# Householder tridiagonalisation: another order for the steps of the last four 128-column blocks

## The chip, the core and the metric

One NeuronCore of a Trainium2 chip runs the whole program; the other cores are idle. The metric is the device time of one execution in microseconds (us). TensorE (PE) multiplies, VectorE (DVE), ScalarE (ACT) and GpSimd (POOL) work elementwise; engines synchronise by semaphores, and each engine takes its own instructions in the order in which they are written.

## The reference

Four graph layers run one after another over `x` (8 x 1024 x 128), each behind a layer norm and relu. The third needs all eigenvectors of a 1024 x 1024 normalised Laplacian:

```
deg = jnp.sum(A, axis=0) + jnp.sum(A, axis=1) - jnp.diagonal(A)
d_inv_sqrt = jnp.where(deg > 0, jax.lax.rsqrt(deg), 0.0)
L = jnp.diag(deg) - A
L_norm = d_inv_sqrt[:, None] * L * d_inv_sqrt[None, :]
_, U = jnp.linalg.eigh(L_norm)
agg = jnp.einsum('mn,bnd->bmd', U.T, features)
h = jax.nn.relu(agg @ W1 + b1)
out = h @ W2 + b2
return jnp.einsum('nm,bmd->bnd', U, out)
```

The other layers are a graph convolution with batch norms, and two attention layers. `eigh` is done in the kernel: reduction to a tridiagonal matrix, eigenvalues by multisection, eigenvectors of the tridiagonal matrix, back transformation.

## The kernel before, in words

The change lies in `tridiagonalise` alone. It removes one column per step with a Householder reflection, 1023 columns, one after another. The matrix `A` stays in SBUF, 128 rows per partition group. Columns go in eight blocks of 128 (`b` = 0 to 7); `T = NT - b` is the number of 128-row tiles that are still active, so T is 8 in the first block and 4, 3, 2, 1 in the last four. A block has four panels of 32 columns (`s` = 0 to 31, `NB_P`); within a panel the matrix itself is not touched, and corrections from the panel's earlier reflections are added instead. At a panel's end TensorE turns the stored vectors and a rank-64 product updates the matrix (L325 to L333, L511 to L518).

Each step is a chain through four engines, held together by semaphores that count steps. In the order of the chain, for the four last blocks:

- `X` (L487) is the new column, and it starts a step. L490 writes the previous step's vector `w`.
- The norm: L430 sums the squares of X per partition into `part`; TensorE sums over partitions with a matrix of ones into `sigma` (in `ring[1]`); ScalarE takes the root, `mu` (L364).
- Scalars (DVE): `rt` = 1/mu, `fl`, `S2` (L449), `pair` (L454), `inv` (L459), `s4` (L468).
- Between them stand the corrections for s > 0: TensorE reads one row of the stored vectors (`rows`) and multiplies X with them (`coefs`); DVE forms `prodb`, `rowsum`, `BnS`, `prodc`, `corr`. Their sizes grow with s.
- The product: TensorE multiplies the matrix with X, `y` (L289, `product(t)` for each tile t), DVE turns it with `tr` (L437) and adds `corr`, which is `t1`, called `tm` (L473).
- Kappa: L476 multiplies `tm`, the scale `s4` and `gx` and sums along the row into `kp`; TensorE sums over the partitions (`kappa`, and `c_sum` once more).
- The end: DVE forms `qa`, `z` (L481), `q` (L483), and with kappa the next X (L487). POOL forms fB, nB and Bc, and ScalarE `sM` and `vm` beside it.

A helper `four` issues each small matmul for four groups of 32 output columns. In the profile each of these counts twice, so one group is x8. The matmuls on `ident16` (L314) write to a bank that nobody reads; there are 8 of them in a step with T = 6 and 10 with T of 5 or less. They stand in TensorE's order between the product and kappa.

```
early = 0 if T < 4 else 1
...
for _ in range(8 if T == 6 else 10):
    nc.tensor.matmul(ring[3][:, 0:P], S["ident16"][:, :], S["ident16"][:, :], start=True, stop=True)
```

Of the kernel before, what the change touches and what calls it, by code (L numbers as in the profile page):

```python
# [11 lines left out]
P = 128  # L12
# [156 lines left out]
XC = N + 5 * NB_P + 1  # L169


def tridiagonalise(nc, S):
# [3 lines left out]
    with ExitStack() as ctx:  # L176
# [11 lines left out]
        eS = sb("eS", [P, NB_P]); tauS = sb("tauS", [P, NB_P]); dS = sb("dS", [P, NB_P]); dq = sb("dq", [P, NB_P]); DS = sb("DS", [P, N])  # L188
# [26 lines left out]
        last_body = len(bodies) - 1  # L215

# [18 lines left out]
        def _(pool):  # L235
# [9 lines left out]
            for k, (b, it0, cnt, s0, s1) in enumerate(bodies):  # L245
                T = NT - b
                with pool.Fori(0, cnt) as it:
                    pool.wait_ge(window_ready, it + (panels_before[k] + 1))
                    for s in range(s0, s1):
# [5 lines left out]
                        pool.wait_ge(Bn_ready, r + 1)  # L255
                        nc.gpsimd.tensor_scalar(fB[:, b:NT], col, fl[:, s:s + 1], None, ALU.mult).then_inc(pool_step, 1)  # L256
                        pool.wait_ge(pool_step, 3 * r + 1)
                        nc.gpsimd.tensor_tensor(nB[:, b:NT], fB[:, b:NT], col, ALU.subtract).then_inc(pool_step, 1)
                        pool.wait_ge(pool_step, 3 * r + 2)
                        nc.gpsimd.tensor_tensor(Bc[:, b:NT], nB[:, b:NT], half_M[:, s, 0:T], ALU.mult).then_inc(pool_step, 1)  # L260
# [5 lines left out]
        def _(pe):  # L266
# [9 lines left out]
            for k, (b, it0, cnt, s0, s1) in enumerate(bodies):  # L276
                T = NT - b
                with pe.Fori(0, cnt) as it:
# [3 lines left out]
                    for s in range(s0, s1):  # L282
# [14 lines left out]
                        early = 0 if T < 4 else 1  # L297
                        for t in range(early):
                            product(t)
# [9 lines left out]
                        for t in range(early, T):  # L309
                            product(t)  # L310
                        if T <= 6:

                            for _ in range(8 if T == 6 else 10):
                                nc.tensor.matmul(ring[3][:, 0:P], S["ident16"][:, :], S["ident16"][:, :], start=True, stop=True)  # L314
                        pe.wait_ge(kappa_part, r + 1)
                        four(kappa(s), half[:, 0:32], kp[:, :]).then_inc(kappa_ready, 1)
                        four(c_sum, half[:, 0:32], kp[:, :], stop=False)
# [28 lines left out]
        def _(act):  # L346
            act.wait_ge(low_ready, 7)
            for k, (b, it0, cnt, s0, s1) in enumerate(bodies):
                T = NT - b
                with act.Fori(0, cnt) as it:  # L350
# [10 lines left out]
                    for s in range(s0, s1):  # L361
# [3 lines left out]
                        act.wait_ge(s4_ready, r + 1)  # L365
                        nc.scalar.activation(sM[:, b:NT], half_M[:, s, 0:T], ACT.Copy, scale=s4[:, s:s + 1]).then_inc(sM_ready, 1)  # L366
# [18 lines left out]
        def _(dve):  # L385
# [14 lines left out]
            for k, (b, it0, cnt, s0, s1) in enumerate(bodies):  # L400
                T = NT - b
                act_t = slice(b, NT)
                with dve.Fori(0, cnt) as it:
# [1573 lines left out]
```

## Time and profile before

| | us |
|---|---|
| Median of 3 runs | 9805.91 (9801.75 to 9810.02) |
| The profiled execution | 9792.26 |
| Its span | 9790.5 |
| Mean granted TensorE clock, whole span | 0.746 of 2.4 GHz |
| DVE busy | 7098.8 (73%) |
| PE busy, modelled | 5600.1 (57%) |

The tridiagonalisation takes the span from about 908 to 6007 us; the last four blocks begin at 3863.1 us. In the rows, the first number of a timeline row is its start in us from the start of the span, and the second its duration; L numbers are lines of the kernel. PE rows are matmuls, PEld their weight loads.

### The profile page before, as it was taken

The numbers are of one execution on the slowest core, as the hardware profiler recorded it, in microseconds if no ns is written. First come the engines' busy times: TensorE is split into PE (matmuls) and PEld (weight loads), VectorE is DVE, ScalarE is ACT, GpSimd is POOL, SyncE is SP. The second block draws the span as 40 slices with busy tenths as digits, with TensorE's granted clock in tenths as the row PEclk, the third lists the DMA queues.
The fourth block names the chain that finished last, engine by engine and source line by source line (L and its number), as shares of the span: only waits on it lengthen the run. The fifth ranks groups of instructions, "written<-read, shape, count | busy, mean of one in ns | idle before, by whom it ended". The sixth has DMA issues, their size and how long they took to land. (4 is left out here: it accounts for less than half of the span.)

```text
span 9790.5 us, 326141 instructions
## 1 busy us (share of the span) xinstructions
PE 5600.1 (57%) x136408; PEld 3949.5 (40%) x136408; DVE 7098.8 (73%) x33446; ACT 1776.4 (18%) x4691; POOL 1185.3 (12%) x5177
## 2 busy tenths in 40 slices
PE   5675888777878777778777764121111110047866
PEld 2354555555566666566656653010000000033355
DVE  3555666767777777777777778989898989954154
ACT  1432111111111111111111111121111110011055
POOL 0000111111222222222222221000000000000000
PEclk8898999999999999786655555555555555579988
DMA  1000000000000000000000000000000000000000
GB/s 35 1 0 18 4 4 4 4 4 4 4 4 4 4 4 4 4 4 4 4 4 4 3 3 2 0 0 0 0 0 0 0 0 0 0 0 1 17 0 17
DMA packets 24594, 41.92 MB, mean 4 GB/s; under 512 B 2464, under 2 KB 20128, under 8 KB 23200
## 3 DMA queue, kind: packets, MB, share of 16 engines
q8 instruction: 1074, 17.60, 0.8%
q1 hardware_dynamic: 23200, 21.70, 0.7%
q14 instruction: 320, 2.62, 0.1%
HBM read 17.50 MB, written 4.19 MB: 2 GB/s over the span
## 5 line engine op out<-in xcount | busy, mean ns | idle before, releaser
L289 PE MATMUL tri_y<-L 128*32 128x256 f32 (+7 forms) x36792 | 1941.3, 343 | 18.7 <-issue 17.7
L289 PEld LDWEIGHTS tri_y<-L 128*32 128x32 f32 x36792 | 1187.9, 122 | 241.9 <-issue 66.3
L1342 PE MATMUL ev_agree<-ev_prod,ev_fold 128*128 128x448 bf16 x520 | 241.3, 567 | 1683.5 <-DVE ev_prod L1465 1666.9
L1342 PEld LDWEIGHTS ev_agree<-ev_prod,ev_fold 128*128 128x128 bf16 x520 | 34.8, 111 | 1887.8 <-DVE ev_prod L1465 1867.4
L314 PE MATMUL tri_ring<-ident 128*128 128x128 bf16 x7414 | 750.3, 268 | 2.1 <-issue 1.9
L1458 DVE SCALAR_TENSOR_TENSOR ev_seq<-ev_seq,ev_ne2G,ev_u 128x112 f32<-128x112 f32 x2048 | 686.1, 335 | 73.3
L1454 DVE SCALAR_TENSOR_TENSOR ev_u<-ev_x,ev_dG,ev_seq 128x112 f32<-128x112 f32 x2048 | 683.9, 334 | 64.0
L272 PE MATMUL tri_k<-tri_kp,tri_half 128*32 128x1 f32 x8176 | 264.8, 189 | 759.7 <-DVE tri_x L476 755.8
L364 ACT ACTIVATE tri_mu<-tri_ring,tri_tiny 128x1 f32<-128x1 f32 x1022 | 267.4, 262 | 2172.6 <-PE tri_ring L272 2172.6
L314 PEld LDWEIGHTS tri_ring<-ident 128*128 128x128 bf16 x7414 | 582.1, 121 | 171.0 <-issue 155.6
L366 ACT ACTIVATE tri_sM<-tri_half_M,tri_s 128x8 f32<-128x8 f32 (+7 forms) x1022 | 304.2, 298 | 1823.4 <-DVE tri_s L468 1823.4
L272 PE MATMUL tri_ring<-L 128*32 128x32 f32 (+25 forms) x35704 | 597.8, 206 | 0.0
L272 PEld LDWEIGHTS tri_k<-tri_kp,tri_half 128*32 128x32 f32 x8176 | 177.6, 120 | 1040.4 <-DVE tri_x L476 1038.8
L256 POOL TENSOR_SCALAR tri_fB<-tri_BnS,tri_fl 128x8 f32<-128x8 f32 (+7 forms) x991 | 303.1, 306 | 2262.2 <-DVE tri_BnS L462 2262.2
L1323 ACT ACTIVATE ev_sgn<-ev_seq 128x1008 bf16<-128x1008 f32 x256 | 267.0, 1043 | 1703.0 <-DVE ev_dummy L1472 1703.0
L440 DVE RECIPROCAL tri_rt<-tri_mu 128x1 f32<-128x1 f32 x1022 | 167.2, 164 | 544.5 <-ACT tri_mu L364 544.5
L437 DVE STREAM_TRANSPOSE tri_tr<-tri_y 128x256 f32<-128x256 f32 (+7 forms) x1022 | 333.7, 326 | 300.6 <-PE tri_y L289 298.2
L272 PEld LDWEIGHTS tri_ring<-L 128*32 128x32 f32 x35704 | 514.4, 118 | 0.2
L272 PE MATMUL tri_p<-L,tri_Hw 128*32 128x2 f32 x8176 | 265.6, 189 | 329.5 <-DVE L L487 188.2
L254 POOL TENSOR_TENSOR tri_xm<-L,tri_Mw 128x8 f32<-128x8 f32 (+7 forms) x1022 | 214.2, 210 | 1404.3 <-DVE L L487 1072.0
L272 PEld LDWEIGHTS tri_p<-L,tri_Hw 128*32 128x32 f32 x8176 | 177.5, 119 | 440.1 <-DVE L L487 278.9
L487 DVE SCALAR_TENSOR_TENSOR L<-tri_vm,tri_k,tri_q 128x8 f32<-128x8 f32 (+7 forms) x1022 | 235.7, 231 | 160.4 <-PE tri_k L272 68.2
(615 smaller groups left out, 12957.9 us busy)
## 6 DMA issues: line engine op xcount, KB each, us to landing
adj<-in_adj_dram SPq DMA_DIRECT2D x12, 1024.0 KB, 8.1
x<-in_x_dram SPq DMA_DIRECT2D x8, 512.0 KB, 7.2
out_dram<-x SPq DMA_DIRECT2D x8, 512.0 KB, 6.6
gcn_w<-in_L_gnn_W_dram SPq DMA_DIRECT2D x2, 128.0 KB, 2.1
spec_w<-in_L_gnn_W_dram SPq DMA_DIRECT2D x2, 64.0 KB, 1.9
dot_wt<-in_L_gnn_W_dram SPq DMA_DIRECT2D x1, 64.0 KB, 1.8
dot_rows<-in_L_gnn_b_lin_dram SPq DMA_DIRECT2D x1, 64.0 KB, 2.7
dot_rows<-in_L_gnn_b_dram SPq DMA_DIRECT2D x1, 64.0 KB, 3.7
```

Of the source, the lines that this page charges most:

```text
L256: nc.gpsimd.tensor_scalar(fB[:, b:NT], col, fl[:, s:s + 1], None, ALU.mult).then_inc(pool_step, 1)
L272: last = nc.tensor.matmul(out[32 * g:32 * g + 32, :], lhsT, rhs, start=start, stop=stop)
L289: last = nc.tensor.matmul(y[32 * g:32 * g + 32, 0:T * 32], A[:, b + t, XC:XC + 1].broadcast_to([P, 32]), cols, start=(t == 0), stop=(t == ...
L314: nc.tensor.matmul(ring[3][:, 0:P], S["ident16"][:, :], S["ident16"][:, :], start=True, stop=True)
L364: nc.scalar.activation(mu[:, :], sigma, ACT.Sqrt, bias=tiny[:, :]).then_inc(root_ready, 1)
L366: nc.scalar.activation(sM[:, b:NT], half_M[:, s, 0:T], ACT.Copy, scale=s4[:, s:s + 1]).then_inc(sM_ready, 1)
L437: return mark(V_.transpose(tr[:, 0:T * 32], y[:, 0:T * 32]))
L487: V_.scalar_tensor_tensor(out=X, in0=vm[:, act_t], scalar=kappa(s), in1=q[:, act_t], op0=ALU.mult, op1=ALU.subtract).then_inc(x_ready, 1)
L1323: nc.scalar.activation(sgn[:, y % 2, :, :], seq[:, y % 2, 1:GRP + 2, :], ACT.Sign).then_inc(sgn_done, 1)
L1342: last = nc.tensor.matmul(agree, fold16[:, :], prod[:, z, h * (GRP // 2):(h + 1) * (GRP // 2), :].rearrange("p s w -> p (s w)"), start=Fal ...
L1454: ku[c] = mark(V.scalar_tensor_tensor(out=u[:, h], in0=xw[:, h], scalar=dG[:, i:i + 1], in1=seq[:, z, s + 1, h], op0=ALU.subtract, op1=ALU ...
L1458: ins = V.scalar_tensor_tensor(out=seq[:, z, s + 2, h], in0=seq[:, z, s, h], scalar=ne2G[:, i:i + 1], in1=u[:, h], op0=ALU.mult, op1=ALU.add)
```

## The change

It touches steps with T of 4 or less (`few(T)`), 511 steps of 1023; code for larger T is as before. In these steps:

- Kappa is no longer summed along the row on DVE. TensorE multiplies `gx` with `tm` for each tile and accumulates, T groups in place of one, and the sum lacks the factor s4/2. That factor is in `vmc` (ACT, from `vm`), used in X, and at a panel's end in `kS`. `c_sum` is T groups of `gx` with `zh` (ACT: tm scaled by s4/2) and the one group with `z`.
- `sigma` is summed a second time, into `sigma_v` in kappa's bank, for DVE. `fl` and a new `sgn2` = sigma_v * sg read it, and stand ahead of `rt`. `aa` = mu * sg + pivot is new, `pair` = rt * sgn2 + aa, and `S2` is gone.
- The norm of the next step stands right behind X, ahead of `w`.
- The turn `tr` stands ahead of `gx` and `s4`. `s4` is two values wide.
- POOL forms `Cf` and `BnS`, DVE `fB`; q is made as (z - column) * half_M in two instructions behind z. `sM`, `nB`, `Bc` and `qa` are gone.
- On TensorE the first tile of the product stands ahead of rows and coefs, behind sigma and sigma_v; for T of 1 and 2 the whole product does. The `ident16` matmuls are 8, 10, 12, 12 for T = 4, 3, 2, 1.

The diff, cut to its core:

```
+FILL = {6: 8, 5: 10, 4: 8, 3: 10, 2: 12, 1: 12}
...
+        sigma_v = kbank[:, NB_P:NB_P + 1]
+        few = lambda T: T <= 4
...
@@ gpsimd
+                        if few(T):
+                            pool.wait_ge(fl_ready, r + 1)
+                            nc.gpsimd.tensor_scalar(Cf[:, b:NT], Cw[:, b:NT, s], fl[:, s:s + 1], None, ALU.mult).then_inc(Cf_ready, 1)
+                            if s:
+                                pool.wait_ge(sum_ready, r + 1 if s0 else r)
+                                nc.gpsimd.tensor_tensor(col, Cw[:, b:NT, s], rowsum[:, b:NT], ALU.add).then_inc(Bn_ready, 1)
...
@@ tensor
+                        first = T if T <= 2 else 1
+                        if not few(T):
+                            for t in range(first):
+                                product(t)
                         pe.wait_ge(norm_part, r + 1)
                         four(sigma, ones[:, 0:32], part[:, :]).then_inc(norm_ready, 1)
+                        if few(T):
+                            four(sigma_v, ones[:, 0:32], part[:, :]).then_inc(norm_again, 1)
+                            for t in range(first):
+                                product(t)
...
+                        if few(T):
+                            pe.wait_ge(gx_ready, r + 1)
+                            pe.wait_ge(t_ready, r + 1)
...
+                            for t in range(T):
+                                last = four(kappa(s), gx[:, b + t:b + t + 1].broadcast_to([P, 32]), tm[:, t0 + t:t0 + t + 1], start=(t == 0), stop=(t == T - 1))
+                            last.then_inc(kappa_ready, 1)
+                            pe.wait_ge(zh_ready, r + 1)
+                            for t in range(T):
+                                four(c_sum, gx[:, b + t:b + t + 1].broadcast_to([P, 32]), zh[:, b + t:b + t + 1], start=(t == 0), stop=False)
...
@@ scalar
+                        if few(T):
+                            act.wait_ge(s4_ready, r + 1)
+                            act.wait_ge(vm_ready, r + 1)
+                            nc.scalar.activation(vmc[:, b:NT], vm[:, b:NT], ACT.Copy, scale=s4[:, s, 1:2]).then_inc(vmc_ready, 1)
...
+                            act.wait_ge(t_ready, r + 1)
+                            nc.scalar.activation(zh[:, b:NT], tm, ACT.Copy, scale=s4[:, s, 1:2]).then_inc(zh_ready, 1)
```

DVE's side is shown by the order of its instructions. First the scalars of a step with T = 1, from `sg` on; before:

```order
L433 TENSOR_SCALAR tri_sg<-tri_p 128x1
L440 RECIPROCAL tri_rt<-tri_mu 128x1
L441 TENSOR_SCALAR tri_fl<-tri_p,tri_ring 128x1
L445 TENSOR_TENSOR tri_prodb<-L,tri_r 128x4
L449 SCALAR_TENSOR_TENSOR tri_S<-tri_rt,tri_ring,tri_mu 128x1
L452 TENSOR_REDUCE tri_rowsum<-tri_prodb 128x1
L454 SCALAR_TENSOR_TENSOR tri_pair<-tri_S,tri_sg,tri_p 128x2
L457 TENSOR_TENSOR tri_prodc<-L,tri_ring 128x4
L459 RECIPROCAL tri_inv<-tri_pair 128x2
```

The same place on DVE after the change (L493 is `rt`, tri_sgn is sgn2):

```order
L487 TENSOR_SCALAR tri_sg<-tri_p 128x1
L489 TENSOR_SCALAR tri_fl<-tri_p,tri_k 128x1
L491 TENSOR_SCALAR tri_sgn<-tri_k,tri_sg 128x1
L493 RECIPROCAL tri_rt<-tri_mu 128x1
L494 SCALAR_TENSOR_TENSOR tri_aa<-tri_mu,tri_sg,tri_p 128x2
L497 TENSOR_TENSOR tri_prodb<-L,tri_r 128x6
L499 SCALAR_TENSOR_TENSOR tri_pair<-tri_rt,tri_sgn,tri_aa 128x2
L502 TENSOR_TENSOR tri_prodc<-L,tri_ring 128x6
L504 TENSOR_REDUCE tri_rowsum<-tri_prodb 128x1
L506 RECIPROCAL tri_inv<-tri_pair 128x2
```

`fl` moved ahead of `rt`, and rowsum behind prodc. Then the end of a step with T = 1 on DVE, from corr to X; before (tri_x, tri_kp is the kappa sum along the row):

```order
L464 TENSOR_REDUCE tri_corr<-tri_prodc 128x1
L468 TENSOR_SCALAR tri_s<-tri_inv,tri_fl 128x1
L469 SCALAR_TENSOR_TENSOR tri_gx<-L,tri_inv,tri_Hw 128x1
L437 STREAM_TRANSPOSE tri_tr<-tri_y 128x32
L473 TENSOR_TENSOR tri_t<-tri_tr,tri_corr 128x1
L476 SCALAR_TENSOR_TENSOR tri_x,tri_kp<-tri_t,tri_s,tri_gx 128x1
L479 TENSOR_TENSOR tri_qa<-tri_t,tri_sM 128x1
L481 SCALAR_TENSOR_TENSOR tri_zS<-tri_t,tri_s,tri_fB 128x1
L483 TENSOR_TENSOR tri_q<-tri_qa,tri_Bc 128x1
L487 SCALAR_TENSOR_TENSOR L<-tri_vm,tri_k,tri_q 128x1
```

The same place on DVE after the change, from corr over X to w (L470 is the norm, L548 is w):

```order
L509 TENSOR_REDUCE tri_corr<-tri_prodc 128x1
L511 STREAM_TRANSPOSE tri_tr<-tri_y 128x32
L517 SCALAR_TENSOR_TENSOR tri_gx<-L,tri_inv,tri_Hw 128x1
L519 SCALAR_TENSOR_TENSOR tri_s<-tri_one_half,tri_inv,tri_fl 128x2
L522 TENSOR_TENSOR tri_t<-tri_tr,tri_corr 128x1
L525 SCALAR_TENSOR_TENSOR tri_fB<-tri_rowsum,tri_fl,tri_Cf 128x1
L533 SCALAR_TENSOR_TENSOR tri_zS<-tri_t,tri_s,tri_fB 128x1
L537 TENSOR_TENSOR tri_q<-tri_zS,tri_BnS 128x1
L539 TENSOR_TENSOR tri_q<-tri_q,tri_half_M 128x1
L543 SCALAR_TENSOR_TENSOR L<-tri_vmc,tri_k,tri_q 128x1
L470 ISA tri_x,tri_part<-L 128x1
L548 SCALAR_TENSOR_TENSOR L<-L,tri_ring,tri_zS 128x2
```

The kappa sum and qa are gone, fB and one of the two q instructions are new, and the norm stands ahead of w. Last, TensorE between the norm and the next step with T = 3; before:

```order
L272 MATMUL tri_ring<-L 32x18 x12
L289 MATMUL tri_y<-L 32x96 x12
L314 MATMUL tri_ring<-ident 128x128 x10
L272 MATMUL tri_k<-tri_kp,tri_half 32x1
L272 MATMUL tri_k<-tri_kp,tri_half 32x1 x3
L272 MATMUL tri_ring<-tri_kp,tri_half 32x1 x4
```

The same stretch of TensorE after the change, from the second sum of the norm on:

```order
L289 MATMUL tri_k<-tri_part,ones 32x1 x4
L306 MATMUL tri_y<-L 32x96 x4
L289 MATMUL tri_r<-L,tri_Hw 32x18
L289 MATMUL tri_r<-L,tri_Hw 32x18 x3
L289 MATMUL tri_ring<-L 32x18 x12
L306 MATMUL tri_y<-L 32x96 x8
L335 MATMUL tri_ring<-ident 128x128 x10
L289 MATMUL tri_k<-tri_t,tri_gx 32x1
L289 MATMUL tri_k<-tri_t,tri_gx 32x1 x11
L289 MATMUL tri_ring<-tri_zh,tri_gx 32x1
L289 MATMUL tri_ring<-tri_zh,tri_gx 32x1 x11
```

A third of the product stands earlier; kappa is 12 matmuls for 4, and c_sum has 12 with zh for the 4 with kp.

## Rows read from the trace of the kernel before

**Rows 1.** The page: the span and the granted clock in 40 equal slices.

```profile
span 9790.5 us, 326141 instructions
PEclk8898999999999999786655555555555555579988
```

**Rows 2.** Busy time in the four last blocks, T = 4, 3, 2, 1.

```profile
core 0: us, PE busy (x) PEld busy (x) DVE busy (x) ACT busy (x) POOL busy (x), PEclk, DMA share, GB/s
3863.10:4438.30 575.20, 435.99 (x15520) 343.99 (x15520) 449.30 (x3092) 103.38 (x427) 140.98 (x640) 0.83 0.02 4
4438.30:4983.30 545.00, 429.65 (x13488) 343.36 (x13488) 425.51 (x3088) 102.48 (x426) 138.62 (x640) 0.67 0.02 4
4983.30:5509.70 526.40, 409.45 (x11456) 327.54 (x11456) 401.59 (x3084) 101.59 (x427) 136.24 (x640) 0.50 0.01 4
5509.70:6007.00 497.30, 348.00 (x9354) 281.94 (x9354) 380.02 (x3059) 99.49 (x417) 132.40 (x635) 0.50 0.01 3
```

**Rows 3.** Timeline of one step, T = 1: start us, duration us, engine, line.

```profile
5700.21 0.22 DVE L487 SCALAR_TENSOR_TENSOR L<-tri_vm,tri_k,tri_q 128x1 f32<-128x1 f32 x1 [0.17 <-PE tri_k L272]
5700.64 0.14 DVE L430 CUSTOM_DVE_ANT_0 tri_x<-L 128x1 f32<-128x1 f32 x1
5700.85 0.29 PE L272 MATMUL tri_ring<-tri_part,ones 128*32 128x1 f32 x8
5701.20 0.26 ACT L364 ACTIVATE tri_mu<-tri_ring,tri_tiny 128x1 f32<-128x1 f32 x1 [1.68 <-PE tri_ring L272]
5701.50 0.16 DVE L440 RECIPROCAL tri_rt<-tri_mu 128x1 f32<-128x1 f32 x1 [0.49 <-ACT tri_mu L364]
5701.58 0.27 DVE L441 TENSOR_SCALAR tri_fl<-tri_p,tri_ring 128x1 f32<-128x1 f32 x1
5701.77 0.18 DVE L445 TENSOR_TENSOR tri_prodb<-L,tri_r 128x34 f32<-128x34 f32 x1
5701.86 0.22 DVE L449 SCALAR_TENSOR_TENSOR tri_S<-tri_rt,tri_ring,tri_mu 128x1 f32<-128x1 f32 x1
5702.12 0.22 DVE L454 SCALAR_TENSOR_TENSOR tri_pair<-tri_S,tri_sg,tri_p 128x2 f32<-128x2 f32 x1
5702.37 0.17 DVE L459 RECIPROCAL tri_inv<-tri_pair 128x2 f32<-128x2 f32 x1
5702.51 0.18 DVE L464 TENSOR_REDUCE tri_corr<-tri_prodc 128x1 f32<-128x34 f32 x1
5702.60 0.20 DVE L468 TENSOR_SCALAR tri_s<-tri_inv,tri_fl 128x1 f32<-128x1 f32 x1
5702.72 0.23 DVE L469 SCALAR_TENSOR_TENSOR tri_gx<-L,tri_inv,tri_Hw 128x1 f32<-128x1 f32 x1
5702.88 0.20 DVE L437 STREAM_TRANSPOSE tri_tr<-tri_y 128x32 f32<-128x32 f32 x1
5703.11 0.16 DVE L473 TENSOR_TENSOR tri_t<-tri_tr,tri_corr 128x1 f32<-128x1 f32 x1
5703.31 0.22 DVE L476 SCALAR_TENSOR_TENSOR tri_x<-tri_t,tri_s,tri_gx 128x1 f32<-128x1 f32 x1
5703.59 0.29 PE L272 MATMUL tri_k<-tri_kp,tri_half 128*32 128x1 f32 x8 [0.89 <-DVE tri_x L476]
5704.00 0.22 DVE L487 SCALAR_TENSOR_TENSOR L<-tri_vm,tri_k,tri_q 128x1 f32<-128x1 f32 x1 [0.16 <-PE tri_k L272]
```

**Rows 4.** Timeline of TensorE, T = 3, a step at half clock.

```profile
4455.49 1.25 PE L314 MATMUL tri_ring<-ident 128*128 128x128 bf16 x10
4456.67 0.29 PE L272 MATMUL tri_k<-tri_kp,tri_half 128*32 128x1 f32 x8
4457.91 0.49 PE L272 MATMUL tri_ring<-L 128*32 128x10 f32 x24
```

**Rows 5.** Timeline of TensorE, T = 2.

```profile
5161.89 0.63 PE L289 MATMUL tri_y<-L 128*32 128x64 f32 x16
```

**Rows 6.** Timeline of TensorE, T = 4, a step at full clock.

```profile
4352.80 0.73 PE L314 MATMUL tri_ring<-ident 128*128 128x128 bf16 x10
```

More of the change, by code:

```diff
@@ L308, in _ @@
                             last.then_inc(coefs_ready, 1)
[L309 removed]
+                        for t in range(first, T):
                             product(t)
[L311 to L317, printed above, removed]
+                        for _ in range(idle(T)):
+                            nc.tensor.matmul(ring[3][:, 0:P], S["ident16"][:, :], S["ident16"][:, :], start=True, stop=True)
+                        if few(T):
+                            pe.wait_ge(gx_ready, r + 1)
+                            pe.wait_ge(t_ready, r + 1)
+                            tm = t1 if s else tr[:, 0:NT * 32].rearrange("p (t m) -> p t m", m=32)[:, :, 0]
+                            t0 = b if s else 0
+                            for t in range(T):
[4 more added lines that the diff above has]
+                                four(c_sum, gx[:, b + t:b + t + 1].broadcast_to([P, 32]), zh[:, b + t:b + t + 1], start=(t == 0), stop=False)
+                        else:
+                            pe.wait_ge(kappa_part, r + 1)
+                            four(kappa(s), half[:, 0:32], kp[:, :]).then_inc(kappa_ready, 1)
+                            four(c_sum, half[:, 0:32], kp[:, :], stop=False)
                         pe.wait_ge(z_ready, r + 1)
@@ L448, in _ @@
-                        after(kk)
-                        kk = mark(V_.scalar_tensor_tensor(out=S2[:, :], in0=rt[:, :], scalar=sigma, in1=mu[:, :], op0=ALU.mult, op1=ALU.add))
-                        if s:
-                            after(k_b)
-                            k_b = mark(V_.tensor_reduce(rowsum[:, act_t], c3(prodb), mybir.AxisListType.XY, ALU.add))
-                        after(kk)
-                        kk = mark(V_.scalar_tensor_tensor(out=pair[:, s, :], in0=S2[:, :].broadcast_to([P, 2]), scalar=sg[:, :], in1=pivot(s), op0=ALU.mult, op1=ALU.add))
@@ L455, in _ @@
-                        if s:
-                            dve.wait_ge(coefs_ready, r + 1 if s0 else r)
-                            k_c = mark(V_.tensor_tensor(c3(prodc), v_w(b)[:, :, :, 0:s], spread(coefs(s)), ALU.mult))
-                        after(kk)
-                        V_.reciprocal(inv[:, :], pair[:, s, :]).then_inc(inv_ready, 1)
-                        if s:
-                            after(k_b)
-                            V_.tensor_tensor(BnS[:, s, 0:T], Cw[:, act_t, s], rowsum[:, act_t], ALU.add).then_inc(Bn_ready, 1)
-                            after(k_c)
-                            k_c = mark(V_.tensor_reduce(corr[:, act_t], c3(prodc), mybir.AxisListType.XY, ALU.add))
```

220 lines of the change are left out of this document (159 added, 61 removed).

## The prediction

> **What bounds the kernel now.** I read the page first for the slices, then busy time block by block, then the timeline of single steps. The page gives a span of 9790.5 us, and a clock row that is near full until about the twentieth slice and at half from the twenty-fourth [rows 1]. The four last blocks, the only ones touched, take 575.2 + 545.0 + 526.4 + 497.3 = 2143.9 us, 22% of the span, and the mean granted clock in them is 0.83, 0.67, 0.50 and 0.50 [rows 2]. As the clock has two levels, 1.2 and 2.4 GHz, the share of time at the lower one is 2 x (1 - mean): 0.34, 0.66, 1 and 1. So there are four blocks under three regimes, and I make the sum for each.
>
> In the last block (T = 1) a step runs from X at 5700.21 to the next X at 5704.00, 3.79 us [rows 3]. The reader is to see a chain with hardly a hole. X to norm takes 0.43 (w stands between), norm to sigma 0.21, sigma to the root 0.35, root to rt 0.30. From rt at 1.29 to kappa's row sum at 3.10, DVE issues one small instruction after another. Then kappa's matmul comes 0.28 after the row sum, and X 0.41 after the matmul. TensorE waits 0.89 for that row sum, so it has room here. Two kinds of distance matter below: an instruction that needs the one before it starts its duration + 0.04 later (t 0.16, next at +0.20; S2 0.22, pair at +0.26), one that doesn't starts 0.08 to 0.19 later (rt to fl 0.08, fl to prodb 0.19, s4 to gx 0.12, gx to tr 0.16) [rows 3].
>
> At T = 3 and half clock it is another picture: the ten idle matmuls begin at 4455.49, take 1.25, and kappa's matmul starts at 4456.67, in their wake [rows 4]. There TensorE's own queue is the path, and whatever is put ahead of kappa on TensorE is paid.
>
> **The new step, T = 1**, in us after X, by distances of [rows 3]. The norm is now directly behind X: 0.22 + 0.04 = 0.26. Sigma 0.47; sigma_v one group later. A group's distance I take from [rows 4]: 24 matmuls last 0.49 and 8 last 0.29, so 0.10 for each further group; with a little for the first, 0.12: 0.59. fl reads sigma_v 0.41 after its matmul (as X does kappa): 1.00. The root, at 0.82 + 0.30 = 1.12, is no longer what is waited for; fl is. Then sgn2 1.19, rt 1.31, aa 1.39, prodb 1.52, pair 1.65 (aa + 0.26), prodc 1.78, rowsum 1.90, inv 2.02, corr 2.10, tr 2.19, gx 2.34, s4 2.49, t 2.61, fB 2.70. The tail is now four dependent instructions: z 0.26 after fB, 2.96; first q 3.22; second q 3.42; X 3.62 (0.20 each behind a 0.16 tensor_tensor). Kappa's matmul would be at 2.61 + 0.28 = 2.89 and allow X at 3.30; vmc (s4 + 0.26, then a ScalarE instruction of about 0.30) allows it near 3.1. So kappa, for which the change is made, stops being the last wait, and the q chain takes its place; from t to X it was 0.89 and will be 1.01. The gain is made ahead of t: 3.79 - 3.62 = 0.17 to 0.20, since the steps that I took at 0.15 (tr to gx, gx to s4) may be 0.12. I take 0.19: 127 x 0.19 = -24 us. Bounds: nothing, if w (below) delays fl by 0.2, and 0.30, if z, q1 and q overlap more than rows of dependent pairs say.
>
> **T = 2, half clock.** The same chain, but both product tiles are now ahead of rows. Their 16 matmuls last 0.63 [rows 5]: sigma_v 0.59, product from 0.71, rows from about 1.30, with DVE 0.41 later at 1.71, where prodb could start at 1.52. That eats 0.17 to 0.19 of the 0.19, and with large s, where rows and coefs take longer, a little more. I take -0.02: 128 x 0.02 = -3 us; bounds -0.15 and +0.10.
>
> **T = 3.** At full clock TensorE has room and DVE's chain holds: -0.18. At half clock, where the path is TensorE's queue [rows 4]: sigma starts 0.12 earlier, sigma_v costs 0.12, the product's place changes nothing, and kappa is three groups instead of one, +0.24. In all +0.24. For large s DVE's corrections take over again (they grow with s) and the step gains 0.10. Half and half: +0.07. Sum: 84 steps x 0.07 = +6, 44 x -0.18 = -8: -2 us.
>
> **T = 4.** Full clock, 84 steps x -0.18 = -15. Half clock, 44 steps: sigma_v +0.12, three more kappa groups +0.34, two idle matmuls fewer -0.25 (1.25 / 10 each, [rows 4]; at full clock 0.73 / 10, [rows 6]), waiting for the norm where a product tile stood before +0.09: +0.30, 44 x 0.30 = +13. Sum -2 us. The case of T = 4 is an estimate from the T = 3 rows.
>
> **What is priced at nothing.** c_sum is late now: it waits for zh, which ScalarE makes after t. At T = 1 zh starts near 2.9, c_sum's groups run from 3.2 to 3.4, and w follows at X + 0.2, behind the norm, which is issued anyway. At T = 4 three more groups put w at X + 0.4 to 0.5; behind w stand sg and fl, and fl waits for sigma_v till 1.00, so 0.5 is covered; without this cover each 0.1 costs 0.1 a step. Rows on TensorE waits for w too, but stands behind a product tile. POOL's Cf and BnS have over 0.7 before they are read. kS and one more link at a panel's end: 16 x 0.07 = +1 us.
>
> **Sum**: -24 - 3 - 2 - 2 + 1 = -30 us. Against the profiled execution, 9792.3 becomes 9762; the median of the runs is 9805.9, 13.6 higher, and becomes 9776.
>
> A rule that weighs the change otherwise: the Trainium skill, "VectorE: DVE Perf Modes", under "The DRAIN you can't avoid", says that the next operation doesn't start until the pipe is empty, that semaphores between operations are free, and that only the number of operations counts. The rows differ: fl starts 0.08 after an rt that lasts 0.16, and a dependent successor 0.20 after t [rows 3]. By the rule the q chain would cost no more than independent instructions, and one instruction fewer a step (the row sum's second half goes) would be worth about 0.08 x 511 = -41 us by itself.
>
> **Rivals.**
> *A, the clock rises.* A step has more matmuls (sigma_v, kappa, c_sum; two more idle ones at T of 1 and 2) in less time. If T = 4 and 3 stay at full clock, the 44 steps at T = 4 gain 0.48 (from +0.30 to -0.18) and the 0.4 that they are now longer than their full-clock neighbours (most of the 0.52 between 1.25 and 0.73 for the idle matmuls, [rows 4, 6]): -39. The 84 at T = 3 gain 0.25 to 0.3: -23. Together -30 - 62 = -92: 9714. For it: the clock already changes level inside these two blocks [rows 2]. Against: T = 3 has TensorE busy for 430 of 545 us at mean clock 0.67, and T = 2 for 409 of 526 at 0.50 [rows 2], so being busy doesn't raise it by itself, and small matmuls may count little. The Trainium skill, "TensorE: Matmul & The Clock Gate", under "The HAM clock gate", has the clock throttled by default and released by activity; by it A would be the expected outcome wherever TensorE's idle time shrinks.
>
> *B, slower: TensorE's queue at T = 4.* Two idle matmuls fewer may tip the block to half clock. Each step that changes from full to half costs 0.48 + 0.4 = 0.88. All 84: +74; the 44 of T = 3: +12; so +86 - 30 = +56: 9862. It decides against the change from 30 / 0.88 = 34 steps on, that is when the share at half clock at T = 4 goes from 0.34 to 0.61. For it: kappa already follows the idle matmuls without a gap [rows 4]. Against: the shorter full-clock step (4%) restores the density that they took away.
>
> *C, no gain.* Either w binds, since fl now stands behind it on DVE and comes ahead of rt, or the new waits cost what was saved. The 0.18 at full clock and at T = 1 shrink to 0 to 0.05: the sum is 0 to -8, or +19 where the half-clock costs (+6, +13) stay: 9798 to 9825, centre 9808. For it: the free time ahead of fl is an inference, as no row shows c_sum with several groups.
>
> **Chances.** Forecast 0.50, A 0.20, B 0.12, C 0.18. A measurement of this kernel can tell 0.2%, 20 us, from no change. Of the forecast's 0.50, whose own range is 9750 to 9795, about 0.07 lies within 20 us; of C 0.12 lies within it and 0.06 above. So faster 0.43 + 0.20 = 0.63, same 0.19, slower 0.18. The range goes from 9705 to 9825: it holds A down to its centre and C, and leaves out most of B.
>
> **What would show it.** In the profile after: norm about 0.26 after X; fl near 1.0 and ahead of rt, with DVE idle before fl (waiting for PE) instead of before rt (waiting for ACT); at T = 1 kappa's matmuls well before X, and DVE's wait on kappa ahead of X gone, the q chain in its place; a step at T = 1 of 3.60 to 3.62 and a last block of about 473 us; at T = 2 prodb waiting for rows, the block at about 524; clocks of 0.83 and 0.67 in the first two. I am wrong if the clock in any block moves by more than 0.05, if X still waits for kappa at T = 1, or if w delays fl.

## The result, and the profile after

The changed kernel takes 10035.51 us (median of 4 runs, 10021.51 to 10055.83), the kernel before 9803.83 beside it: ratio 1.0242, 95% interval 1.0218 to 1.0266. It is slower by 232 us. The forecast was 9776, its range 9705 to 9825.

The page after, to be held against [rows 1]: 240.0 us more span, 11% more instructions, and a clock that falls one slice earlier (the 16th).

```profile
span 10030.5 us, 360888 instructions
PE 5987.8 (60%) x153038; PEld 4340.2 (43%) x153038; DVE 7186.2 (72%) x32953; ACT 1928.3 (19%) x5202; POOL 1093.0 (11%) x4650
PEclk8898999999999997666655555555555555579978
```

Busy time of the four last blocks after, which answers to [rows 2]:

```profile
3855.30:4626.80 771.50, 621.17 (x22432) 507.70 (x22432) 484.60 (x2968) 141.52 (x554) 116.04 (x508) 0.64 0.02 4
4626.80:5254.50 627.70, 527.15 (x18608) 437.07 (x18608) 452.71 (x2964) 140.47 (x553) 115.45 (x508) 0.59 0.02 4
5254.50:5773.40 518.90, 467.52 (x14784) 412.10 (x14784) 419.42 (x2960) 139.58 (x555) 114.02 (x508) 0.50 0.02 4
5773.40:6253.00 479.60, 398.99 (x10636) 332.46 (x10636) 385.48 (x2938) 136.87 (x544) 109.89 (x504) 0.50 0.01 4
```

Measured from the start of one block to that of the next, T = 4 went from 575.1 to 771.5 (+196.4), T = 3 from 545.0 to 627.8 (+82.8), T = 2 from 526.4 to 518.8 (-7.6), T = 1 from 502.6 to 480.0 (-22.6). A block whose code is the same in two kernels varies between profiles: by 25 us at T = 5 (611.8 to 636.9), by under 8 us at T of 4 and below. So the two last blocks did what was forecast (-3, -24), and the loss is all in the first two (forecast -2 and -2). The DVE column grows little there; what grows is TensorE's count of instructions: (22432 + 22432) / 128 = 350 a step at T = 4, where [rows 2] give 243. The granted clock went from 0.83 to 0.64 at T = 4 and from 0.67 to 0.59 at T = 3.

TensorE's timeline after, T = 4, in the record that answers to [rows 6]:

```profile
4111.21 0.43 PE L289 MATMUL tri_k<-tri_t,tri_gx 128*32 128x1 f32 x32
4112.69 0.41 PE L306 MATMUL tri_y<-L 128*32 128x128 f32 x8
4114.08 0.62 PE L335 MATMUL tri_ring<-ident 128*128 128x128 bf16 x8
4115.06 0.23 PE L289 MATMUL tri_k<-tri_t,tri_gx 128*32 128x1 f32 x4 [0.36 <-DVE tri_t L522]
4115.91 0.39 PE L289 MATMUL tri_k<-tri_t,tri_gx 128*32 128x1 f32 x26 [0.62 <-issue]
4116.93 0.24 PE L289 MATMUL tri_ring<-tri_part,ones 128*32 128x1 f32 x8
4117.36 0.38 PE L289 MATMUL tri_ring<-L 128*32 128x24 f32 x20
4119.65 0.36 PE L289 MATMUL tri_ring<-L 128*32 128x24 f32 x10 [1.92 <-issue]
4119.89 1.47 PE L306 MATMUL tri_y<-L 128*32 128x128 f32 x22
```

The reader is to see the last but one row. Coefs is 32 matmuls in a row on one wait; after 20 of them TensorE does nothing for 1.92 us and then goes on with the same operation. No semaphore stands there, and the trace names no releaser ("issue"). The same happens inside kappa at 4115.91. I counted such stretches (over 0.3 us, within a TensorE operation or with no releaser) over a block's panels: 84 at T = 4, 111.8 us in all; 65 at T = 3, 67.6 us; none in either block before. I call them dry stretches. The other engines wait for them, as the waits of the T = 4 block show (engine, line, what it waited for, us in total, times, longest):

```profile
DVE tri_tr L511 <- PE tri_y L306: 88.2, 109, 2.6
PE tri_ring L289 <- issue: 47.6, 32, 1.9
DVE tri_prodc L502 <- PE tri_ring L289: 46.7, 41, 2.1
```

The first row isn't made of dry stretches alone: DVE's turn `tr` waits for the product in 109 steps, more than there are stretches. In the same block before it hardly waited:

```profile
DVE tri_tr L437 <- PE tri_y L289: 1.2, 7, 0.2
```

What runs dry can be read from the DMA view. The queue "q8 instruction" brings TensorE's instructions from memory: in e3_pad84 below, where nothing but TensorE instructions was added to the kernel before, the T = 1 block had 153 of its packets for 76. In the T = 4 block (the columns are packets, MB, share of 16 engines) it brought after, in 737 us:

```profile
q8 instruction: 176, 2.88, 1.6%
```

and before, in 575 us:

```profile
q8 instruction: 126, 2.06, 1.5%
```

A packet is 16.4 KB, and by 31040 matmuls and loads for 126 packets it holds some 250 of them. A step with 352 needs 1.4 packets. In the stretch of the timeline above they began at 4105.6, 4109.5, 4113.5, 4117.4, 4121.3, 4125.3 and 4128.6 and took about 1 us each: one every 3.4 to 4.0 us, where 84 instructions a us would need one every 3.0.

At T = 1 the new step is much as forecast; to be held against [rows 3]:

```profile
5951.34 0.22 DVE L543 SCALAR_TENSOR_TENSOR L<-tri_vmc,tri_k,tri_q 128x1 f32<-128x1 f32 x1
5951.60 0.16 DVE L470 CUSTOM_DVE_ANT_0 tri_x<-L 128x1 f32<-128x1 f32 x1
5952.28 0.28 DVE L489 TENSOR_SCALAR tri_fl<-tri_p,tri_k 128x1 f32<-128x1 f32 x1 [0.16 <-PE tri_k L289]
5952.61 0.15 DVE L493 RECIPROCAL tri_rt<-tri_mu 128x1 f32<-128x1 f32 x1
5953.76 0.15 DVE L522 TENSOR_TENSOR tri_t<-tri_tr,tri_corr 128x1 f32<-128x1 f32 x1
5954.05 0.29 PE L289 MATMUL tri_k<-tri_t,tri_gx 128*32 128x1 f32 x8
5954.10 0.22 DVE L533 SCALAR_TENSOR_TENSOR tri_zS<-tri_t,tri_s,tri_fB 128x1 f32<-128x1 f32 x1
5954.51 0.16 DVE L537 TENSOR_TENSOR tri_q<-tri_zS,tri_BnS 128x1 f32<-128x1 f32 x1 [0.19 <-DVE tri_zS L533]
5954.71 0.16 DVE L539 TENSOR_TENSOR tri_q<-tri_q,tri_half_M 128x1 f32<-128x1 f32 x1
5955.00 0.22 DVE L543 SCALAR_TENSOR_TENSOR L<-tri_vmc,tri_k,tri_q 128x1 f32<-128x1 f32 x1
```

The norm is 0.26 after X, fl 0.94 and ahead of rt and waiting for TensorE, kappa's matmul 0.95 before X, and the q chain is last (X shows no wait). The mean step at T = 1 inside the panels is 3.57 us (3.79 before; 3.62 forecast).

### The profile page after: what moved, and what is told of

Read it like the earlier page. It is cut to its first block and busy times, and to the rows that moved or that the text cites. A ratio compares the mean times of both kernels' runs of the same rounds, so it can differ in the third digit from the quotient of the medians.

```text
span 10030.5 us, 360888 instructions
## 1 busy us (share of the span) xinstructions
PE 5987.8 (60%) x153038; PEld 4340.2 (43%) x153038; DVE 7186.2 (72%) x32953; ACT 1928.3 (19%) x5202; POOL 1093.0 (11%) x4650
## 5 line engine op out<-in xcount | busy, mean ns | idle before, releaser
L306 PE MATMUL tri_y<-L 128*32 128x256 f32 (+7 forms) x36792 | 2053.5, 351 | 82.9 <-issue 82.0
L306 PEld LDWEIGHTS tri_y<-L 128*32 128x32 f32 x36792 | 1232.0, 125 | 315.0 <-issue 137.1
L335 PE MATMUL tri_ring<-ident 128*128 128x128 bf16 x7668 | 824.3, 280 | 20.4 <-issue 20.4
L335 PEld LDWEIGHTS tri_ring<-ident 128*128 128x128 bf16 x7668 | 645.8, 127 | 195.8 <-issue 175.6
L404 ACT ACTIVATE tri_vm<-tri_xm,tri_inv 128x8 f32<-128x8 f32 (+7 forms) x1022 | 296.4, 290 | 772.1 <-DVE tri_inv L506 772.1
L557 DVE STREAM_TRANSPOSE tri_tr<-tri_y 128x256 f32<-128x256 f32 (+3 forms) x511 | 202.6, 396 | 289.7 <-PE tri_y L306 287.6
L289 PE MATMUL tri_k<-tri_kp,tri_half 128*32 128x1 f32 x4088 | 124.0, 181 | 418.0 <-DVE tri_x L596 417.8
L401 ACT ACTIVATE tri_sM<-tri_half_M,tri_s 128x8 f32<-128x8 f32 (+3 forms) x511 | 153.0, 299 | 1040.0 <-DVE tri_s L588 1040.0
L289 PEld LDWEIGHTS tri_k<-tri_kp,tri_half 128*32 128x32 f32 x4088 | 80.5, 108 | 580.0 <-DVE tri_x L596 579.3
L289 PE MATMUL tri_r<-L,tri_Hw 128*32 128x2 f32 (+16 forms) x7936 | 297.7, 219 | 25.9 <-issue 25.3
```

What stands on the lines that cost most here:

```text
L289: last = nc.tensor.matmul(out[32 * g:32 * g + 32, :], lhsT, rhs, start=start, stop=stop)
L306: last = nc.tensor.matmul(y[32 * g:32 * g + 32, 0:T * 32], A[:, b + t, XC:XC + 1].broadcast_to([P, 32]), cols, start=(t == 0), stop=(t == ...
L404: nc.scalar.activation(vm[:, b:NT], xm[:, b:NT], ACT.Copy, scale=inv[:, 1:2]).then_inc(vm_ready, 1)
L557: return mark(V_.transpose(tr[:, 0:T * 32], y[:, 0:T * 32]))
```

## The experiments

The theory that I formed (**theory 1, supply**): TensorE's instructions arrive at some 67 to 69 a us; a step that asks for more waits for them. Rivals: **theory 2**, the execution time or the clock of the added matmuls; **theory 3**, waits between the engines in the new code. Step means below are those inside the panels. The ratios are to the kernel before, run beside each.

**The change at T of 2 and 1 alone** (e1_few2).

```
-        few = lambda T: T <= 4
+        few = lambda T: T <= 2
```

The idle matmuls at T = 4 and the order of the product at T = 3 are put back too, as before.

> The change at T = 2 and 1 alone; T = 4 and 3 as before. In the changed kernel the mean step is 3.84 us for 3.89 at T = 2 and 3.57 for 3.79 at T = 1. Theory 1 (supply: TensorE's instructions arrive no faster than about 64 a us, and only T = 4 and 3 ask for more): the two blocks keep this gain, 124 x 0.05 + 123 x 0.22 = 33 us, so about 9770. Theory 2 (the clock: the changed blocks leave TensorE at half clock and the rest is dragged along): T = 4 and 3 are at their old clocks and T = 2 and 1 were at half clock anyway, so 9770 too. Theory 3 (late c_sum or w, in every changed step): the loss belongs to each changed block, also 2 and 1, and some of the +232 stays: over 9830.

9766.33 us, ratio 0.9966 (0.9952 to 0.9979): faster by 0.3%. Steps 3.825 at T = 2 and 3.57 at T = 1; T = 4 and 3 are back (569.0, 547.6). Theory 3 falls for these two blocks.

**Kappa and c_sum as one matmul of 128 columns per tile** (e2_wide), which takes 12 of 16 instructions away for each tile and sum: 96 of 352 in a step at T = 4 and 72 of 292 at T = 3.

```
-    last = four(kappa(s), gx[...].broadcast_to([P, 32]), tm[...], ...)
+    last = nc.tensor.matmul(kappa(s), gx[...].broadcast_to([P, P]), tm[...], ...)
```

> The changed kernel, with kappa's and c_sum's groups of gx each as one matmul of 128 output columns instead of four of 32. This takes 6 of 8 instructions for each tile and sum: at T = 4 a step has about 256 TensorE instructions instead of 352, at T = 3 about 204 for 276. TensorE's own time for them grows or stays. Theory 1 (supply, 64 a us): the floor of a step falls from 5.5 to 4.0 us at T = 4 and from 4.3 to 3.2 at T = 3, the gaps of 1 to 2 us inside the stream go, T = 4 comes to 4.1 to 4.5 and T = 3 to 3.8 to 4.2: total 9760 to 9820. Theory 2 (TensorE's time at half clock): no less work, so T = 4 stays above 5.5 us and the total at 10000 or more.

(At T = 4 the trace has 256 instructions a step, as stated; at T = 3 it is 220 for 292.) 10246.38 us, ratio 1.0449 (1.0432 to 1.0466). The dry stretches were gone, none in either block, but the time was not: steps 6.147 and 5.152. The total is where theory 2 had it, and theory 1's 9760 to 9820 was missed by over 400 us. TensorE's timeline, kappa and c_sum at T = 4:

```profile
4115.46 1.84 PE L343 MATMUL tri_k<-tri_t,tri_gx 128*128 128x1 f32 x8
4117.16 0.99 PE L347 MATMUL tri_ring<-tri_zh,tri_gx 128*128 128x1 f32 x4
```

Kappa's four matmuls of 128 output columns take 1.84 us at half clock and 1.02 at full clock; the 16 of 32 columns in the changed kernel take 0.61 and 0.43 (medians of the block). So I had put one cost in the place of another: the run shows that fewer instructions end the stretches, and says nothing of what they cost.

**28 and 84 one-column matmuls added to the kernel before at T = 1** (e3_pad28, e3_pad84).

```
+                        if T == 1:
+                            for g in range(28):      # 84
+                                nc.tensor.matmul(ring[3][32 * (g % 4):32 * (g % 4) + 32, 0:1], S["ident16"][:, 0:32], S["ident16"][:, 0:1], start=True, stop=True)
```

> The kernel before, with 28 matmuls of one column (bf16, 32 output columns, into the bank that nobody reads) added in each step at T = 1, where TensorE waits 0.9 us for kappa's row sum. A step then has about 148 + 56 = 204 TensorE instructions. Theory 1 (supply): 204 / 64 = 3.2 us, under the 3.79 of the step: no change, within 10 us of before. Theory 2 (TensorE's time): 28 x 0.015 = 0.4 us inside the 0.9 us: no change either.

> As e3_pad28 with 84 such matmuls: about 148 + 168 = 316 TensorE instructions a step at T = 1. Theory 1 (supply, 64 a us): 316 / 64 = 4.9 us for a step of 3.79, 127 steps: +145 us, with idle stretches of TensorE that nothing in the program explains. Theory 2 (TensorE's time, 0.015 us each by the eight in 0.12 us of a small group): 1.26 us in a gap of 0.9: at most +0.36 x 127 = +46 us, and no unexplained idle stretches.

28 (204 instructions a step): 9802.31 us, 1.0002 (0.9990 to 1.0014), nothing. 84 (316): 9890.74 us, 1.0089 (1.0072 to 1.0105), step 4.55 to 4.58, which is 316 / 69. The expected +145 came as +92 by the medians, since the instructions came at 69 a us and not at 64. TensorE's timeline there:

```profile
5706.09 0.31 PE L289 MATMUL tri_y<-L 128*32 128x32 f32 x8
5706.33 0.29 PE L314 MATMUL tri_ring<-ident 128*128 128x128 bf16 x1
5708.02 1.14 PE L314 MATMUL tri_ring<-ident 128*128 128x128 bf16 x9 [1.40 <-issue]
5709.10 0.82 PE L317 MATMUL tri_ring<-ident 128*32 128x1 bf16 x84
```

All 84 take 0.82 us. But the wait here is in another operation, 1.40 us behind the first of the ten idle matmuls and ahead of those added in this step. An execution cost would sit where the matmuls are. Over the block the waits without a releaser are spread over coefs, rows, the product, the idle and the added matmuls; inside the steps they add up to 96 us, as much as the block lost.

**Thin idle matmuls** (e4_thin): as many instructions as after, a sixteenth of their columns at T of 4 and 3.

```
+                            fw = 8 if T in (3, 4) else P
+                            nc.tensor.matmul(ring[3][:, 0:fw], ..., S["ident16"][:, 0:fw], ...)
```

> The changed kernel, with the idle matmuls at T = 4 and 3 over 8 columns instead of 128; their number, and so the number of TensorE's instructions (352 and 292 a step), is the same. Theory 1 (supply of instructions): the number decides, so T = 4 and 3 keep their long steps, within 0.3 us of 5.8 and 4.7, and the total stays within 60 us of the changed kernel's 10035. Theory 2 (TensorE's time at half clock): 8 x 0.11 = 0.9 us a step goes at T = 4 and 10 x 0.11 = 1.1 at T = 3: 0.9 x 128 + 1.1 x 128 = up to -250 us, total near 9800 to 9850.

10051.64 us, 1.0253 (1.0235 to 1.0270), as slow as after; steps 5.888 and 4.696. TensorE's waits in the T = 4 block:

```profile
PE tri_ring L289 <- issue: 40.8, 35, 2.1
PE tri_y L306 <- issue: 22.7, 22, 1.9
PE tri_k L289 <- DVE tri_t L523: 62.0, 118, 0.8
```

Theory 2 in its simple form (TensorE is full of work) falls: work was taken away and nothing came back. The run isn't as clean as I planned it, since the granted clock fell with the idle columns, to 0.52 at T = 4 and 0.50 at T = 3 (0.64 and 0.59 in the changed kernel), which could have eaten a gain. But at the same level it holds: steps wholly at half clock and without a stretch took 5.14 at T = 4 and 4.22 at T = 3, against 5.05 and 4.23. The third row says why: kappa now waits for `tm` in 118 steps, so the idle matmuls no longer kept it.

**The change at T of 3 and below** (e5_few3: `few = lambda T: T <= 3`).

> The change at T = 3, 2 and 1, with T = 4 as before. T = 3 has 292 TensorE instructions a step where before had 212; at 67 a us (what e3_pad84 showed: 316 in 4.58 us is 69) that is 4.35 us, over the 4.03 of before. Theory 1 (supply, each block by itself): about +0.65 us x 128 = +83 us against e1_few2's 9766, so near 9850. Theory 2 (a clock that T = 4 drags down into T = 3): T = 3 is as cheap as forecast once T = 4 is restored, 9765 to 9775.

9850.96 us, 1.0046 (1.0031 to 1.0060), as theory 1 had it; T = 3 step 4.712, block 631.4, T = 4 back at 575.7. The two losses are separate, one per block.

**c_sum's tile groups taken from TensorE** (e6_cdve): DVE adds kappa times s4/2 to a c_sum of one group. 288 and 244 instructions a step. The same at T of 3 and below is e7_cdve3.

```
-                            for t in range(T):
-                                four(c_sum, gx[...], zh[...], start=(t == 0), stop=False)
+                            V_.tensor_scalar(kc[:, :], kappa(s), c4h, None, ALU.mult)
...
+                            V_.tensor_scalar(cs[:, :], c_sum, kc[:, 0:1], None, ALU.add)
```

> The changed kernel without c_sum's T groups of gx on TensorE and without zh: DVE makes kappa times s4/2 in one instruction ahead of X and adds the z part in one behind the norm. TensorE has 288 instructions a step at T = 4 (352 in the changed kernel), 244 at T = 3 (292), 200 at T = 2 and 152 at T = 1. Theory 1 (supply, 67 a us): floors of 4.3, 3.6, 3.0 and 2.3 us, so T = 4 falls from 5.8 to 4.4 to 4.7 and T = 3 from 4.7 to about 4.0: total 9780 to 9830. Theory 2 (TensorE's time): the groups taken out stand behind kappa and before the next pivot, off the path, and take 0.4 us; the total stays above 9950.

> As e6_cdve, but with T = 4 as before; 244, 200 and 152 TensorE instructions a step at T = 3, 2 and 1, all with floors under their steps. Theory 1: the part that the forecast had right is kept and T = 3 adds to it: T = 3 at 3.85 to 4.0 for 4.03, total 9740 to 9765, faster than e1_few2's 9766 or the same. If the two added DVE instructions lie on the path, 0.1 us x 380 steps = 38 us are lost and it is no better than before, 9790 to 9800.

e6: 9883.56 us, 1.0081 (1.0066 to 1.0095). Some 150 us of the 232 come back (152 by the medians, 158 by the ratios) with 64 and 48 instructions fewer a step. T = 3 is nearly cured (4.091, with one stretch), T = 4 is not: 4.998, with 51 stretches and 43.9 us. I had expected 9780 to 9830, as 288 / 4.2 us = 69 a us seemed just possible. e7: 9768.13 us, 0.9959 (0.9946 to 0.9972), just above the 9740 to 9765 expected and no better than e1: at T = 3 the new step is then free of the loss but gains nothing (4.082, 4.033 before).

**The idle matmuls as wide ones** (e8_wfill on e6, e9_few2w on e1): 2 or 3 of 512 columns for 8 to 12 of 128.

```
+                            n4 = min(4, left)
+                            nc.tensor.matmul(ring[3][:, 0:n4 * P]..., S["ident16"][:, :], S["ident16"][...].broadcast_to([P, n4, P]), ...)
```

> As e6_cdve, with the idle matmuls made wide: the same columns in one instruction for up to 512 columns instead of 128, so 2 for 8 and 3 for 10 or 12. A step has 276 TensorE instructions for 288 at T = 4, and 230 for 244 at T = 3. Theory 1 (supply): T = 4, which had gaps in the stream in e6_cdve (5.00 us a step), gains at least 12 / 64 = 0.2 us, 25 us in all; T = 3, which had none, gains nothing; near 9855. Theory 2 (columns on TensorE set the time or the clock): the columns are the same, no change against e6_cdve.

> As e1_few2 (the change at T = 2 and 1), with the idle matmuls wide at all T of 6 and less. The kernel before asks for 276 instructions in 4.47 us at T = 5, 62 a us, just under the supply of 67 to 69. Theory 1: where gaps of the supply already cost something at T = 5 and 6, 14 instructions fewer (262) give back up to 0.1 to 0.2 us a step: 9740 to 9766, the fastest kernel if so; at T = 4 and below nothing. Theory 2: no change against 9766. A loss is possible if one wide matmul keeps kappa's group waiting longer.

e8: 9839.85 us, 1.0039 (1.0023 to 1.0054); T = 4 step 4.912, stretches 36.6 us. The step gained 0.09 us over e6 where at least 0.2 was expected, and one profile of each doesn't part that from nothing. e9: 9744.15 us, 0.9947 (0.9934 to 0.9961), the fastest of all, 0.5% under the kernel before. Its interval overlaps that of e1, and its steps at T of 5 and 6 are unchanged, so what the wide form adds to e1 isn't established. It has 14 instructions fewer at T = 5, and the gain of 0.1 to 0.2 us a step that theory 1 allowed there did not come.

**The number alone, at T = 4** (e10_t4pad28 with 300 instructions, e11_t4pad54 with 352, the same as after): the kernel before, with the one-column matmuls of e3 there, 28 or 54 of them.

> The kernel before with 28 one-column matmuls (56 instructions) added in each step at T = 4 between the idle matmuls and kappa: 300 TensorE instructions a step for 244, nothing of the change in it. Theory 1 (supply, a block of 256 in 3.6 to 3.8 us): 300 ask for at least 4.3 to 4.5 us, more where they come unevenly; T = 4 rises from 575 to 600 to 650 us, with gaps. Theory 2 (another part of the change makes T = 4 slow): only TensorE's time, 0.4 us in the third of the steps in which it is the path, 0.4 x 44 = 18 us at most, 575 to 593, no gaps.

> As e10_t4pad28 with 54 such matmuls: 352 TensorE instructions a step at T = 4, as many as the changed kernel has there. Theory 1: the block comes near the changed kernel's 771 us, 710 to 790, and the total to 9950 to 10010. Theory 2: 0.8 us of TensorE's time on the path in at most every step, mostly covered at full clock: 610 to 660 us, total below 9890.

e10: 9828.78 us, 1.0019 (1.0008 to 1.0031); step 4.443, block 596.5 (+21), just under theory 1's 600 to 650, but with 43 stretches of 31.1 us, which theory 2 didn't have. e11: 9916.36 us, 1.0102 (1.0077 to 1.0126); step 5.169, block 692.3 (+117), 77 stretches of 73.7 us, at a clock of 0.72. It lies between the two theories, under the 710 to 790 of the one and over the 610 to 660 of the other. TensorE's waits in its T = 4 block:

```profile
PE tri_ring L272 <- issue: 33.7, 38, 1.7
PE tri_y L289 <- issue: 28.2, 26, 1.7
```

Nothing of the change is in this kernel but the number, and the wait without a releaser is there, most of it in the same two operations. Of the 117 us 73.7 are stretches. Part of the rest is the added matmuls' own time, so theory 2 had a part too: in steps wholly at half clock and without a stretch, set against steps of the kernel before at the same place in the panel, e11 is 0.54 us longer (3 places), and the 54 matmuls take 0.57 there; at full clock it is 0.01 (6 places).

The runs side by side. "Asked" is instructions by the step that would be had without the loss (that of the kernel before, or the forecast one):

| kernel, T | instructions | asked, per us | step, us | stretches, us |
|---|---|---|---|---|
| after, T=1 | 168 | 47 | 3.57 | 0 |
| e3_pad28, T=1 | 204 | 54 | 3.79 | 0 |
| after, T=2 | 232 | 60 | 3.84 | 1.6 |
| e6, T=3 | 244 | 61 | 4.09 | near 0 |
| before, T=5 | 276 | 62 | 4.47 | 10.6 |
| before, T=6 | 304 | 63 | 4.80 | 17.7 |
| e8, T=4 | 276 | 66 | 4.91 | 36.6 |
| e6, T=4 | 288 | 69 | 5.00 | 43.9 |
| e10, T=4 | 300 | 71 | 4.44 | 31.1 |
| after, T=3 | 292 | 73 | 4.70 | 67.6 |
| e3_pad84, T=1 | 316 | 83 | 4.56 | 96 |
| e11, T=4 | 352 | 83 | 5.17 | 73.7 |
| after, T=4 | 352 | 84 | 5.78 | 111.8 |

At T of 1, 2, 5 and 6 pauses at the panels' ends have no releaser either; for T of 1 and 2 the table leaves them out, and of before's 10.6 and 17.7 us only 2.5 and 6.0 lie inside steps. So the kernel before already had a few dry stretches, in its blocks with the most instructions.

**The stretches and the packets together.** Three readings of the kept traces tie the stretches to the loading.

- *Where they fall.* In the T = 1 block of e3_pad84, 109 stretches lie within an operation. From one to the next TensorE starts a whole multiple of 256 instructions, to the instruction, in 105 of 108 cases. In e11 it is so in 69 of 72; after the change, at T = 4, in 75 of 78 to within 4. The other three of each lie across a panel's end. That fits what a packet holds by the count above.
- *When they end.* Of the same 109, 108 end 1.2 to 1.6 us after a packet has landed, and 78 of 79 at T = 4 after the change. The stretch of 1.92 us shown above ended at 4119.65; the packet that began at 4117.36 had landed at 4118.32.
- *How far the loading runs ahead.* In 139 blocks of 256 instructions of e3_pad84 exactly one packet began during each, 1.04 to 1.74 us after the block's first instruction. It took about 1.0 us, and the next block began 1.2 us or more after it had landed. No block took less than 3.47 us.

So what a stretch waits for is the next 256 instructions, and in e3_pad84 the limit is one of time per block: 256 / 3.47 = 74 a us at best, with nothing saved up while TensorE waits for DVE. In e10 and after the change 95% of the blocks that I could place took over 3.3 us, in e11 over 3.0.

**The steps of T = 4 by clock and by stretch.** Means in us, with the number of steps; steps in which the clock changed, and those at full clock with a stretch, are left out.

| kernel | clock of the block | full clock, no stretch | half clock, no stretch | half clock, with a stretch |
|---|---|---|---|---|
| before | 0.83 | 4.09 (79) | 4.49 (9) | none |
| e10 | 0.84 | 4.23 (47) | 4.67 (10) | 5.38 (1) |
| e11 | 0.72 | 4.17 (8) | 5.04 (21) | 6.06 (4) |
| e6 | 0.71 | 4.09 (32) | 4.95 (14) | 6.13 (15) |
| after | 0.64 | 4.11 (8) | 5.05 (17) | 6.55 (23) |

The change thus has a second cost: its half-clock step at T = 4 is 0.56 us longer even where nothing runs dry, where the prediction had 0.30. In these 17 steps `tr` waits 0.72 us a step for the product, whose first tile now stands behind sigma and sigma_v; in the 9 of before it waits 0.11.

## Why the prediction was wrong

**The step that failed** is the costing of added TensorE instructions in the terms T = 4 and T = 3. It priced them by execution alone (0.12 or 0.10 for a group) and said "At full clock TensorE has room"; that each step would have to bring 352 instructions for 244, and 292 for 212, was never counted, and no term stood for waiting for them. The term T = 4 was -2 us and measured +196, T = 3 -2 and +83. The numbers to see it were in [rows 2]: dividing the counts there by the blocks' time gives 54 a us at T = 4, and the change asked for 84. What no row of before gave is where the limit lies; e3_pad84 shows one, at T = 1, far from the change. That the dry stretches come from the number of instructions and not from their work is shown by e4 (less work, the same loss), by e11 and by where the stretches fall.

**A second step failed, in the T = 4 term.** At half clock it took kappa's place behind the idle matmuls as the path and came to +0.30 a step. Measured without stretches it is +0.56, the path runs over the product and `tr`, and far more than 44 steps stand at half clock. The loss of 196 us at T = 4 comes out as an estimate from the rows above: 112 for the stretches; the share at half clock, 2 x (1 - mean), rose from 0.34 to 0.72, 49 steps x 0.94 (5.05 - 4.11) = 46; the 44 steps that were there before, x 0.56 = 25. Together 183.

**T = 1** (-24): right, -22.6. Its links erred both ways and partly cancelled: fl and t came a little sooner (t at 2.42 for 2.61), while z to the first q took 0.32 to 0.41 for 0.26 and the second q to X 0.29 for 0.20. By the rival view that only the number of DVE instructions counts these links would have been as short as those between independent neighbours, 0.07 from rt to aa and 0.09 from gx to s4 in the same step; they weren't.

**T = 2** (-3): -7.6, a little better than forecast, and more than chance: unchanged T = 2 blocks took 521.1 to 528.5 us in five profiles, changed ones 515.6 to 519.0 in four. The wait that I named did not come: prodb hardly waits for rows, though the product of 16 matmuls took 0.63 as in [rows 5]. X waited for kappa by over 0.15 us in 9 steps only.

**T = 3 at half clock**, kappa behind the idle matmuls, holds as a mechanism, if one looks at a step without a dry stretch. TensorE's timeline after, answering to [rows 4]:

```profile
4790.23 1.25 PE L335 MATMUL tri_ring<-ident 128*128 128x128 bf16 x10
4791.41 0.50 PE L289 MATMUL tri_k<-tri_t,tri_gx 128*32 128x1 f32 x24
```

Kappa follows without a gap and lasts 0.50 for 0.29: +0.21, forecast +0.24. But the term took only +0.07, because it let DVE's corrections win for large s. Set against steps of before at the same place in the panel, half-clock steps without a stretch are 0.26 longer (14 places), for large s no less than for small. At full clock the gain was 0.09 (6 places) at T = 3 and 0.11 (5 places) at T = 4, for 0.18. These are few steps, and small beside the stretches.

**What was priced at nothing**: w did not delay fl, and rival C was not seen at T = 1. Rival A had the clock wrong: it fell in both blocks, while TensorE had more matmuls than before. Rival B came true in part. The share at half clock at T = 4 passed its 0.61 (0.72), and its price of 0.88 for a step that falls to half clock is near the 0.94 measured. Its reason, the two idle matmuls fewer, isn't enough: e11 has all ten and fell to 0.72. In these runs the low clock goes with dry stretches; whether they alone bring it down isn't shown, and e4 shows that fewer idle columns do too. B was part of the loss, some 46 us by the estimate above, and not the larger one.

The Trainium skill, "Runtime: NRT & Kernel Launch", under "Instruction fetch mechanics", says that an engine's instructions are streamed in blocks of 16 KiB (256 instructions), and that crossing a block is "mostly hidden". The trace agrees with the blocks (16.4 KB, about 250); it doesn't with the second part, as TensorE stands still for 73.7 us in 128 steps of e11, at those crossings.

**What stays open.** A mean rate isn't the rule. Over a block e3_pad84 got a packet every 3.7 us (153 in 570), e11 every 3.9 (179 in 692), after every 4.2 (176 in 737) and e6 every 4.5 (141 in 637), all with dry stretches. That one packet begins per block of 256 explains why a pause earns nothing for the burst that follows. It doesn't explain why, after the change and in e6, some packets began up to 3.9 us after the block's first instruction, and I have no run on that. That e10 asks for more than e6 and e8 and runs faster is mostly the clock (0.84 against 0.71 and 0.72) and the costlier half-clock step, as the table by clock shows. What brings the clock down is open.

## What to carry to other kernels

When a change adds many small instructions to one engine, divide that engine's instructions by the time, before and as planned, and look at the busiest comparable stretch of the trace: on this TensorE small steps with up to about 60 a us ran freely, and from about 66 on none did. The mean is only a first sign, as 256 instructions in a row seldom came here in less than 3.4 us; count the densest 256. One call of `four` is 16 instructions, cheap in busy time and dear in supply; moving a handful of values to a vector engine bought back some 150 us. Idle time that begins in the middle of one operation, with no releaser, is the sign to look for, at distances of 256 instructions, and the cure is fewer instructions, if they don't each cost more. A second habit: sort the steps by granted clock and by stretch before giving a loss one cause.

## What the runs showed of the hardware that was not expected

- TensorE's instruction stream gave at most about 69 instructions a us over a block of steps (e3_pad84: 316 in 4.56 us). Dry stretches lasted up to 2.0 us, 1.3 on average after the change and 0.8 in e3_pad84.
- They fall between blocks of 256 instructions (105 of 108 distances in e3_pad84) and end 1.2 to 1.6 us after a packet has landed. One packet began in each such block, at least 1.04 us after its first instruction.
- An fp32 matmul with 128 output columns and one moving column takes about 0.25 us at full and 0.46 us at half clock (e2_wide, 1.02 and 1.84 us for four). A sum wanted on all partitions was cheaper as four strips of 32 (0.43 and 0.61 us for the same four tiles).
- Ten idle matmuls of 128 columns or their like in matmuls of 512 gave the same step (4.406 in e9 and 4.395 in e1 at T = 5).
